# One of a head's sixteen probability tiles transposed by TensorE instead of VectorE, in a macaron attention layer

## What is computed

```python
content_score = jnp.einsum('bhsp,bhtp->bhst', q + u, k)
pos_score = _relative_shift(jnp.einsum('bhsp,htp->bhst', q + v, pos))
weights = jax.nn.softmax((content_score + pos_score) / jnp.sqrt(jnp.float32(P)), axis=-1)
out = jnp.einsum('bhst,bhtp->bhsp', weights, val)
```

## Time and profile before

| | |
|---|---|
| median of three runs | 432.4 us |
| the profiled execution's own time | 432.4 us |
| its span, first to last instruction | 430.6 us |
| busy share of the span: DVE | 91% |
| PE (matmuls) | 82% |
| ACT | 61% |
| POOL | 41% |
| TensorE clock granted, mean | 0.97 |

### The profile page before, as it was taken

How to read it: one execution, slowest core, us unless ns; L and a number is a source line. 1 busy time by engine, 2 the same in 40 slices (tenths; PEclk the granted TensorE clock), 3 DMA queues, 4 the chain that set the end, 5 groups by cost and what they waited for, 6 DMA issues and landing times.

```text
span 430.6 us, 18108 instructions
## 1 busy us (share of the span) xinstructions
PE 351.8 (82%) x7344; PEld 288.4 (67%) x7344; DVE 392.2 (91%) x565; ACT 264.1 (61%) x642; POOL 176.0 (41%) x216
## 2 busy tenths in 40 slices
PE   1887798785989788897888978889798897984893
PEld 1666675663878677686776867768687686961683
DVE  8879888459999999999999999999999999958695
ACT  1687365336566666666666666666666666633990
POOL 7444756549313415144150431505325053204562
PEclk9999899988899999999999999999999999996899
DMA  7004257574221323213132131322313242010002
GB/s 220 1 2 174 70 144 233 145 203 113 42 70 35 83 45 69 72 34 82 34 73 66 38 81 30 78 64 40 80 22 87 67 76 36 23 52 2 0 26 73
DMA packets 58853, 31.01 MB, mean 72 GB/s; under 512 B 35470, under 2 KB 57454, under 8 KB 58702
## 3 DMA queue, kind: packets, MB, share of 16 engines
q1 hardware_dynamic: 57470, 29.18, 26.5%
q0 software_dynamic: 672, 0.49, 0.8%
q10 hardware_dynamic: 672, 0.80, 0.7%
HBM read 19.44 MB, written 10.88 MB: 70 GB/s over the span
## 4 chain that ended last, share of the span: by engine, by line
DVE 55%; issue 20%; PE 12%; ACT 5%; POOL 3%; SPq 2%; DVEq 1%; DMA 0%; POOLq 0%; ACTq 0%
DVE pT L989 27%; DVE negmax L975 19%; PE pair L1097 2%; DVE xh L796 2%; DVE sqsum L908 1%; PE pair L1055 1%; PE pair L1243 1%; ACT v_rep L679 1%; ACT v_rep L691 1%; DVE x L922 1%; POOL grs L521 1%; PE pair L1199 1%; DVE stat L786 1%; DVE pT L956 1%; PE pair L1284 1%
## 5 line engine op out<-in xcount | busy, mean ns | idle before, releaser
L727 ACT ACTIVATE probs<-pair,negmax 128x512 f32<-128x512 f32 x256 | 173.9, 684 | 104.7 <-DVE negmax L975 104.7
L975 DVE TENSOR_REDUCE negmax<-pair 128x2 f32<-128x1024 f32 x128 | 152.1, 1188 | 6.3 <-PE pair L1216 6.3
L989 DVE STREAM_TRANSPOSE pT<-probs 128x1024 f32<-128x1024 f32 x128 | 157.0, 1227 | 0.4 <-ACT probs L727 0.4
L1199 PE MATMUL pair<-stage_k,stage_c 128*32 128x512 f16 x1024 | 115.5, 399 | 33.0 <-ACT probs L727 30.0
L1205 PE MATMUL pair<-stage_z,stage_q 128*32 128x512 f16 x1024 | 112.5, 387 | 0.0
L584 POOL TENSOR_TENSOR xh<-rowsum,xh 128x16 f32<-128x16 f32 x15 | 43.6, 2904 | 162.8 <-ACT probs L727 162.8
L1216 PE MATMUL pair<-stage_z,stage_q 128*32 128x446 f16 (+59 forms) x1024 | 102.0, 282 | 0.0
L1211 PE MATMUL pair<-stage_z,stage_q 128*32 128x488 f16 (+56 forms) x1024 | 99.5, 278 | 0.0
L1243 PE MATMUL pair<-pT,v_diag 128*32 128x128 f32 (+1 forms) x2176 | 90.5, 267 | 0.0
L1199 PEld LDWEIGHTS pair<-stage_k,stage_c 128*32 128x32 f16 x1024 | 52.6, 140 | 46.3 <-ACT probs L727 36.2
L1243 PEld LDWEIGHTS pair<-pT,v_diag 128*32 128x32 f32 x2176 | 69.3, 111 | 2.1
(11 more groups left out here) (118 smaller groups left out, 366.4 us busy)
## 6 DMA issues: line engine op xcount, KB each, us to landing
stage_z<-z_scratch SPq DMA_DIRECT2D x16, 254.0 KB
stage_q<-qs_scratch SPq DMA_DIRECT2D x116, 24.0 KB
qs_scratch<-pT SPq DMA_DIRECT2D x9, 256.0 KB, 2.6
stage_z<-z_scratch SPq DMA_DIRECT2D x16, 128.0 KB
kc_scratch<-pT SPq DMA_DIRECT2D x8, 256.0 KB
stage_z<-z_scratch SPq DMA_DIRECT2D x16, 127.5 KB
stage_c<-qc_scratch SPq DMA_DIRECT2D x61, 32.0 KB
stage_k<-kc_scratch SPq DMA_DIRECT2D x15, 128.0 KB
```

The source lines that it names most:

```text
L727: nc.scalar.activation(probs[:, q % 6, :], score_pair(q // 2)[:, q % 2, :], ACT.Exp, bias=negmax[:, q % 8:q % 8 + 1], accum_out=rowsum[:, ...
L975: nc.vector.tensor_reduce(negmax[:, 2 * n % 8:2 * n % 8 + 2], score_pair(n)[:, :, :], AX.X, ALU.max, negate=True).then_inc(max_ready, 1)
L989: nc.vector.transpose(pT[:, par, 2 * n:2 * n + 2, :].rearrange("p a s -> p (a s)"), probs[:, 2 * n % 6:2 * n % 6 + 2, :].rearrange("p a s ...
L1199: mm(bank[32 * j:32 * j + 32, :], all_rows[:, 32 * j:32 * j + 32], stage_k[:, par, :], start=True, stop=False, skip_group_check=True)
```

## The change

Tile 9 (`PE_TILE`, the second of pair 4) of every head but the last is no longer transposed by DVE. `turn(h, par, 4)` takes one tile, 128x512, instead of two. On TensorE, right after the scores of tile 15, `turn_tile` transposes tile 9 out of `probs`: 16 x 4 matmuls in float32, each with a 32x32 block of probs as the stationary operand and a 32x32 block of the identity as the moving one, on the four diagonal 32x32 tiles of the array (rows 32j, columns 32j). They fill the whole bank `ps[4 + par]`, into which the value products of the same head go later. ACT copies the bank into pT's slot 9 after the exp of tile 15.

New waits: PE ahead of tile 15's scores for the exp of tile 9 and for `o_ready` of head h-2; ACT ahead of the exp of tile 15, which overwrites tile 9 in probs, for `tile_turned`; PE ahead of values(h, kb = 0) for `tile_copied`. DVE's hardware loop is one turn shorter, and heads 14 and 15 are unrolled.

```diff
-            def exp_tile(h, q):
+            def exp_tile(h, q, par):
+                by_pe = q == NQ - 1 and not (isinstance(h, int) and h == H - 1)
+                if by_pe:
+                    act.wait_ge(tile_turned, h + 1)
...
                                      accum_out=rowsum[:, bass.ds(h * NQ + q, 1)]).then_inc(probs_ready, 1)
+                if by_pe:
+                    nc.scalar.activation(pT[:, par, PE_TILE, :], ps[4 + par], ACT.Copy).then_inc(tile_copied, 1)
...
-                nc.vector.transpose(pT[:, par, 2 * n:2 * n + 2, :].rearrange("p a s -> p (a s)"),
-                                    probs[:, 2 * n % 6:2 * n % 6 + 2, :].rearrange("p a s -> p (a s)"))\
+                count = 1 if n == PE_TILE // 2 and not (isinstance(h, int) and h == H - 1) else 2
+                nc.vector.transpose(pT[:, par, 2 * n:2 * n + count, :].rearrange("p a s -> p (a s)"),
+                                    probs[:, 2 * n % 6:2 * n % 6 + count, :].rearrange("p a s -> p (a s)"))\
...
-            with dve.Fori(0, (H - 4) // 2) as it:
+            with dve.Fori(0, (H - 6) // 2) as it:
                 for k in range(2):
                     head(it * 2 + (4 + k), k)
+            head(H - 2, 0)
+            head(H - 1, 1)
...
                     pe.wait_ge(pT_ready, h * NP + q1 // 2)
+                    if not (isinstance(h, int) and h == H - 1):
+                        pe.wait_ge(tile_copied, h + 1)
...
+            def tile_ready(h):
+                if not (isinstance(h, int) and h < 2):
+                    pe.wait_ge(o_ready, h - 1)
+                pe.wait_ge(probs_ready, h * NQ + (PE_TILE + 1))
+
+            def turn_tile(par):
+                for kb in range(KB):
+                    for j in range(4):
+                        r, c = slice(32 * j, 32 * j + 32), slice(32 * kb, 32 * kb + 32)
+                        ins = mm(ps[4 + par][r, c], probs[r, PE_TILE % 6, c], ident[r, r], start=True, stop=True,
+                                 skip_group_check=True)
+                ins.then_inc(tile_turned, 1)
...
                 for q in range(NQ):
+                    by_pe = q == NQ - 1 and not (isinstance(h, int) and h == H - 1)
+                    if by_pe:
+                        tile_ready(h)
                     scores(h, par, q)
+                    if by_pe:
+                        turn_tile(par)
                     if not first and q >= LAG:
                         values(h - 1, 1 - par, q - LAG)
```

More of the change, by code:

```diff
@@ L59 @@
 LOADS = 16
+PE_TILE = 9
 def macaron_kernel(nc, ins, out):
@@ L223, in macaron_kernel @@
         pT_ready = sem("pT_ready")
+        tile_turned = sem("tile_turned")
+        tile_copied = sem("tile_copied")
         av_ready = sem("av_ready")
@@ L739, in _ @@
                 for q in range(NQ):
-                    exp_tile(h, q)
+                    exp_tile(h, q, h % 2)
             for h in range(2, 4):
                 for q in range(NQ):
-                    exp_tile(h, q)
+                    exp_tile(h, q, h % 2)
                     if q == 3:
@@ L748, in _ @@
                     for q in range(NQ):
-                        exp_tile(it * 2 + (4 + k), q)
+                        exp_tile(it * 2 + (4 + k), q, k)
                         if q == 3:
```

## The result

The kernel after takes 460.75 us (median of four runs, 454.32 to 464.12) against 432.49 us before (431.8 to 432.74). By these medians it is 28 us slower, where 8 us faster was forecast. Every ratio in this document goes by the fast runs alone, those within 1.5% of a kernel's fastest (454.32 and 460.3 us after), and here it is 1.058, with an interval of 1.053 to 1.062. The profiled execution is the one of 464.12 us, the slowest of the four.

The account below looks back on a forecast made before the run. DVE was taken to bound the kernel; 15 half transposes saving 0.53 us each give 8.0 us, with PE and ACT staying ahead: 432.4 - 8.0 = 424.4 us. The range was 423.1 to 433 us.

Parts of the forecast that it names:

- What bounds the kernel: Step on the kernel before: DVE ends the ring, 18.06 us a head, so whatever DVE is relieved of is gained.
- What DVE is relieved of: Step on DVE: fifteen transposes halved to 512 elements save 0.53 us each, 8.0 us in all, at most 8.6.
- Rival 3: On DVE: the half transpose costs like the whole one, so 432.4 us stays; chance 0.03.
- What turn_tile takes: Step on PE: 128 records at 7.3 ns, 0.93 us, plus 0.35 us for two changes of the array's shape: 1.3 us.
- T: Time on PE of turn_tile with all it brings: 1.3 us taken, room for 1.57, no gain left at 2.10.
- Rival 2: In turn_tile: the four diagonal tiles do not run side by side or hinder one another in one bank; 458 us, chance 0.19.
- The sign that the prediction named: Forecast is wrong if DVE waits for PE at every head's opening reduce, the wait's length being T - 1.57.
- What PE has room for: Step on PE between tile 15 and the next head's tile 0: turn_tile may take 1.57 us before DVE waits.
- the ring DVE, ACT, PE, DVE: Cycle of waits among the three engines that sets a head's period: 18.06 us before, 17.53 forecast.
- Waits and the other engines: Step on new waits and ACT: they delay nothing; ACT's copy of 0.60 us fits its 0.98 us hole.
- Head 0: Side effect: the turn fills 1.3 us of PE's 3.01 us idle hole; may save up to 0.65 us, counted only in the low end.
- Chances and range: Faster 0.70, same 0.10, slower 0.20; range 423.1 to 433 us, leaving out the slow rival at 0.19.

Follow-up runs that it names:

- e7: The kernel before with TensorE's hardware loop written out, heads 3 to 14 one after another, nothing else changed; 432.68 us in one run.
- e10: The kernel before with 20 idle matmuls a head in TensorE's loop and 64 more ahead of the loop; 431.33 us in one run.
- e8: The changed kernel (whole turn on TensorE) with TensorE's hardware loop written out; 434.91 us in ten runs, ratio 1.004.
- e11: The changed kernel with TensorE's loop written out and PE turning only the last 8 of tile 9's 16 blocks; 427.58 us, ratio 0.991.
- e5: The kernel before with 20 idle one-column matmuls added to each looped head on TensorE, body 1653 instructions; 451.96 us in one run.
- e9: The kernel before with 32 idle matmuls ahead of TensorE's loop, the loop's body unchanged; 446.01 us in one run.
- e6: The kernel before with 50 idle one-column matmuls added to each looped head on TensorE, body 1773 instructions; 448.79 us in one run.
- e3: The kernel before with 110 idle one-column matmuls added to each looped head on TensorE, body 2013 instructions; 473.11 us in one run.

## Why the prediction was wrong, and where it was right

**What bounds the kernel.** Right for the kernel before: e7 and e10, which have DVE's work unchanged and PE's supply intact, stand at before's time.

**What DVE is relieved of.** Right. The half transpose has a record of 0.69 us, and from its start to the next reduce's is 176.12 - 175.50 = 0.62 us, where the whole one took 1.15: 0.53 saved, as taken. Rival 3 is out.

**What turn_tile takes.** Right in sum. Timeline of PE at the end of head 13 in e8 (tile 15's scores, the turn, the values), where no block's edge breaks the turn:

```profile
342.98 0.41 PE L1211 MATMUL pair<-stage_k,stage_c 128*32 128x512 f16 x4
343.76 1.29 PE L1274 MATMUL pair<-ident,probs 32*32 32x32 f32 x128
344.97 1.80 PE L1257 MATMUL pair<-pT,v_diag 128*32 128x128 f32 x54
```

The last of the 128 records starts 1.29 - 0.194 = 1.10 us after the first, 8.6 ns each where 7.3 was forecast. From the first of them to the first value matmul is 344.97 - 343.76 = 1.21 us, which holds one change of shape. T, which holds both, is how much later the values start behind tile 15: 344.97 - 342.98 = 1.99 us against 12.76 - 12.10 = 0.66 in the prediction's reading of before, so 1.33 us, and 1.3 was taken. The two changes of shape cost some 0.2 us (1.33 less 128 x 8.6 ns), less than the 0.35 taken; the small matmuls a little more than forecast.

**Rival 2.** Its mechanism is refuted by the same lines: four diagonal tiles that write one bank, at 8.6 ns a record, ran side by side. The rule of the Trainium skill in TensorEngine Tiling (Array Packing), Restrictions and Gotchas, that different row tiles cannot access one PSUM bank simultaneously, did not hold here, and the about 25 ns between starts of the Trainium skill's TensorE: Matmul & The Clock Gate (section "Wait — 56ns, not 53.3ns?") did not hold between tiles. That its 456 to 461 us fit the measured 460.75 is chance: both are DVE waiting for PE, but it placed a wait of 1.6 us in every head, and the trace has 4 to 6 us at six places. The sign that the prediction named was that DVE waits for PE at the opening reduce of every head, by T - 1.57. In after DVE does wait at the openings of heads 2 to 15, but by anything from 0.24 to 6.21 us, where a T of 1.33 gives no wait at all; in e8 heads 4 and 8 open without one.

**What PE has room for.** This is the step that failed. It added T to PE's path and let everything else on PE stand as it was: tile 0 of the next head would follow the values at once. But T was measured in time on the array, and the turn also brings 256 instructions a head, 512 in each body of 1571. No part of the prediction counted instructions; "the array and neither the weight loads nor the issue" was read from streams that a loaded program had fed. The condition that broke is outside the ring DVE, ACT, PE, DVE altogether, and no rival had it. What the runs put in its place is 26.55 us at the five jumps and 6.21 us behind the broken turn of head 14, and some 7 us of smaller waits: 1.09 and 1.23 us at the openings of heads 2 and 3, 0.24 to 1.55 us at those of the even heads from 4 on, and 1.8 us more than before in head 0. Against them stand 8 us of relief. With its instructions there in time the step holds: in e8 heads 3 and 7, whose next openings wait for nothing, have periods of 17.56 and 17.57 us, and 17.53 was forecast.

**Waits and the other engines.** Right as far as it went. ACT's copies:

```profile
L738 ACT ACTIVATE pT<-pair 128x512 f32<-128x512 f32 x15 | 8.9, 593 | 0.0
```

593 ns each, where 0.60 us was taken, and DVE's transposes wait 0.4 us for exps in the whole span. In the clean heads nothing of it is late.

**Head 0.** Not shown. The period of head 0 is 17.91 us (18.20 before), and DVE's stops of 0.43 and 0.22 us are gone. But they are gone in e7 too, with a period of 17.45 us, and its first three heads are those of the kernel before. So this differs from one execution to the next without the turn.

**Chances and range.** The range ended at 433, and its rivals all lay in the turn's time, none in the supply of instructions. No run has the whole turn with its instructions in time in every head: e8 with its 434.9 is above the range too, by the burst. Nearest is e11 with half the turn, forecast by the same sum at 432.5 - 4.1 = 428.5, measured 427.58.

## What to carry to other kernels

Beside the time that an edit adds to an engine, count the instructions it adds to the engine's hardware loop, and see on the page how often the instruction queue fetches: packets about equal to the program's size in blocks mean a loop that stays loaded, and a loop near the limit can be tipped by 82 instructions in its body (e5), or by 65 ahead of it (e9). If time is lost mainly at the jump back, write the loop out before giving up the change. Many tiny matmuls in a row are dear in instructions even where they are cheap on the array: cut the burst until the waits with no releaser are gone.

## What the hardware showed that I had not expected

- TensorE's instructions come in packets of 16,384 bytes, one for 256 instructions; 27, 58 and 73 packets answer to 27.7, 58.4 and 73.6 blocks run through in before, e7 and e8.
- A loop that touches 7 such blocks is fetched once (before, e10); one that touches 8 or 9 was fetched again at its jumps back in all eight kernels that have one (in e9 at two of five), with 1.9 to 8.1 us of delay for DVE at each (e6, e3). Size alone does not decide: 1571 instructions missed in e9 and 1653 stayed in e10.
- Code without a jump is fetched ahead with no loss at 5.9 us a block (e7), but where 256 instructions go within 1.1 us there are gaps of 0.6 to 2.0 us at the edges of blocks (e8).
- In a loop that isn't kept PE can also stop at the edge of its last block, without a jump: for 3.84 us in after, for 7.8 in e3.
- Four 32x32 tiles on the array's diagonal, all writing one PSUM bank, start a record every 8.6 ns.
- Behind a hole of 4.89 us PE is granted 0.57 of its clock for the next four microseconds.
